# A selective-scan kernel: every fourth product delta\*u\*B by a broadcast load and GpSimd, in place of TensorE and VectorE

## The chip, the cores and the metric

The kernel runs on one core of one Trainium2 chip. The metric is device time in microseconds of one execution of the whole program. Three timed runs of the kernel before gave 1536.02 us as the median (1535.4 to 1540.58).

## The reference: what is computed

For 4096 tokens of width 256, float32 throughout:

```python
xn = layernorm(x)
left, right = split(layernorm(xn)*gamma + beta) @ W_up + b_up        # 128 channels each
u     = silu(causal_conv3(left));  delta = softplus(u @ W_delta + b_delta)
Bm, Cm = u @ W_B, u @ W_C                                             # 64 states each
# for every token t, channel d, state n:
h[d,n] = exp(delta[d]*A[d,n]) * h[d,n] + (delta[d]*u[d]) * Bm[n]      # recurrence over t
y[d]   = sum_n h[d,n] * Cm[n]
s = xn + ((y + u*D) * silu(right)) @ W_down + b_down
g = silu(top-2-of-8 mixture of experts of xn, hidden width 1024)
out = x + s * g
```

The recurrence has 128 x 64 independent sequences over 4096 steps.

## The kernel before, in words

**Pairs and chunks.** The 4096 tokens are cut into 8 chunks of 512 (numbered 0 to 7). Two of the 128 channels times 64 states fill the 128 partitions, so a chunk has 64 pairs of channels, and the main loop runs over 512 pairs `s`. For each pair:

1. ScalarE's queue loads delta of the two channels, each row repeated over 64 partitions, by a broadcast DMA from DRAM (`load_delta`, line 530, three pairs ahead). ScalarE writes exp(delta\*A) to one of two PSUM banks (line 614).
2. TensorE "spreads" delta\*u of the two channels over the partitions: one 128x512 matmul of a 0/1 matrix `pick` with `stack`, which holds delta\*u in two parts (`spread`, line 1117), to one of two PSUM banks `du_bank`. VectorE multiplies that by B (`mult`, line 866), into one of two slots of `b_ring`.
3. VectorE scans: h = a\*h + b along the 512 tokens (`scan`, line 876), into a ring of 8.
4. GpSimd multiplies h by C (`state_by_c`, line 394), into a ring of 8. For 14 pairs of chunk 0 VectorE does it (line 912).
5. TensorE sums over the states, four pairs at a time (`reduce_quad`, line 1052).

**Experts.** The mixture of experts is cut into 39 tiles of 256 rows, 35 of them live with this data. A tile is nine "turns": one that transposes its rows (line 1089) and eight steps. In a step TensorE makes gate and up (line 1105) and three steps later the output product (line 1074, `LAG = 3`); ScalarE makes tanh and a copy (lines 551, 553); VectorE the gated half (line 888); GpSimd the product `hid` (line 409). After each tile ScalarE evicts the sum (line 560) and GpSimd scatters it by two indirect DMAs (line 415). A schedule written out in Python, `BY_PAIR`, gives each pair its turns: 315 live turns over pairs 62 to 483, so three pairs of four have one; from pair 484 on the four dead tiles, up to two turns per pair, with a tiny matmul (line 1041) in place of the products but ScalarE, VectorE and GpSimd working as before.

**The next chunk's inputs** are made meanwhile, at fixed places of a chunk's 64 pairs: convolution at 11 to 13, silu at 16 to 18, softplus and the split of delta\*u at 19 to 29, all mostly on VectorE (lines 709 to 762); at 32 SyncE stores them to DRAM (`store_parts`, five DMAs), at 36 it loads `stack`. The previous chunk's y is gated at pair 5 and projected down at 6 to 10 (lines 895 to 904, 1061).

**Order.** Each engine executes its instructions in the order written. At pair `s` VectorE does mult(s), scan(s-1), then the gated half of pair s-1's turn; TensorE does spread(s+1), a reduction when s%4 is 3, then the turn; GpSimd does state_by_c(s-1), then `hid` of pair s-1's turn and, once per tile, the scatters; ScalarE does load_delta(s+3), exp(s), then its part of the turn. All waits are on semaphores.

Of the kernel before, what the change touches and what calls it, by code (L numbers as in the profile page):

```python
# [6 lines left out]
P = 128  # L7
T, D, E, I, N = 4096, 256, 8, 1024, 64
NT = T // P
CH = 512  # L10
NC = T // CH
TC = CH // P
PAIRS = P // 2
# [66 lines left out]
BY_PAIR = turns_by_pair()  # L80


def state_on_vector(s):

    return s % 4 == 2 and s < 2 * NT - SCATTERS_FIRST
# [19 lines left out]
def mamba_and_experts(nc, x, gam, bet, w_up, b_up, conv_w, conv_b, w_dl, b_dl, w_b2, w_c2, a_log,  # L105
                      dvec, w_dn, b_dn, gate, w_all, c_ident, c_upper, c_pick, c_win, c_first,
                      c_start, c_token, out):
    with ExitStack() as ctx:
# [3 lines left out]
        def sem(name):  # L112
            return ctx.enter_context(nc.semaphore(name))

        x_sorted = nc.dram_tensor("x_sorted", [TILES * SLOT, ROW], F32).ap()
        results = nc.dram_tensor("results", [2 * T + PADS * P, D], F32).ap()
        delta_d = nc.dram_tensor("delta_d", [P, T], F32).ap()
        parts_d = nc.dram_tensor("parts_d", [2, P, T], F32).ap()
        tails_d = nc.dram_tensor("tails_d", [P, 2, T], F32).ap()

# [62 lines left out]
        def stage(name):  # L183

            return spare[:, dict(cv=0, dlt=0, thl=1, ud=1, thr=2, sr=2, u=3, hi=3, ex=4, ln=5, lo=5, wm=6, du=6)[name], :]

        def of_chunk(rep, c, at):

            return rep[:, :, :].rearrange("p c t -> p (c t)")[:, c * (CH + 2) + at:c * (CH + 2) + at + CH]

        def cols(c):

            return slice(c * CH, (c + 1) * CH)
# [32 lines left out]
        s_dp, s_bc, s_bcev, s_sp, s_dlt = (sem(k) for k in ("s_dp", "s_bc", "s_bcev", "s_sp", "s_dlt"))  # L226
        s_partd = sem("s_partd")
        s_stack = [sem("s_stack0"), sem("s_stack1")]
        s_dl = [sem(f"s_dl{i}") for i in range(D_RING)]
        s_tails, s_sel, s_exp, s_bm, s_scan = (sem(k) for k in ("s_tails", "s_sel", "s_exp", "s_bm", "s_scan"))  # L230
        s_carry, s_hc, s_hcv, s_red, s_gt2, s_gated = (sem(k) for k in ("s_carry", "s_hc", "s_hcv", "s_red", "s_gt2", "s_gated"))
# [10 lines left out]

        CONSTS = 19
        KD = 7
        STORES = 16 * 5

        def ge(eng, s, n):

            if n > 0:
                eng.wait_ge(s, n)  # L250
# [5 lines left out]
        def _(sp):  # L256
# [22 lines left out]
            def store_parts(c):  # L279

                sp.wait_ge(s_dlt, (c + 1) * KD)
                sp.dma_start(delta_d[:, cols(c)], stage("dlt")).then_inc(s_partd, 16)
                for n, name in enumerate(("hi", "lo")):
                    sp.dma_start(parts_d[n, :, cols(c)], stage(name)).then_inc(s_partd, 16)
                sp.dma_start(tails_d[:, 0, cols(c)], stage("sr")).then_inc(s_partd, 16)
                sp.dma_start(tails_d[:, 1, cols(c)], stage("ud")).then_inc(s_partd, 16)

            def load_stack(c):

                sp.wait_ge(s_partd, STORES * (c + 1))  # L290
                ge(sp, s_sel, PAIRS * (c - 1))
                for n in range(2):
                    sp.dma_start(stack[64 * n:64 * n + 64, c % 2, :, :].bitcast(F32),
                                 parts_d[n, :, cols(c)].rearrange("(j c) t -> c j t", c=64)).then_inc(s_stack[c % 2], 16)
# [17 lines left out]
            for s in range(PAIR_COUNT):  # L312
                c, at = s // PAIRS, s % PAIRS
                if at == TAILS_AT:
                    sp.wait_ge(s_lr, NC)
                    ge(sp, s_dn, 2 * c)
                    sp.dma_start(tails[:, :, :], tails_d[:, :, cols(c)]).then_inc(s_tails, 16)
                for name, cc, r in work_at(s):
                    if name == "store":
                        store_parts(cc)  # L320
                    elif name == "stack":
                        load_stack(cc)
                if s == MOE_FIRST - 8:
                    sp.wait_ge(s_ytr, NC)
                    sp.wait_ge(s_table, 1)
                    load_weights(0)
                for turn, i, k in BY_PAIR[s]:
                    if turn == "step" and k == 0 and i:
                        load_weights(i)
                if s == (NC - 1) * PAIRS + 12:  # L330
                    sp.wait_ge(s_bm, (NC - 1) * PAIRS)
                    sp.wait_ge(s_hc, states((NC - 1) * PAIRS - 1, False))
                    sp.wait_ge(s_partd, STORES * NC)
                    for c in range(NC):
                        sp.dma_start(x_again[c], x[0, cols(c), :].rearrange("(n p) c -> p n c", p=P)).then_inc(s_again, 16)
# [29 lines left out]
        def _(pool):  # L365
# [21 lines left out]
            def state_by_c(s):  # L387

                c = s // PAIRS
                if s % PAIRS == 0:  # L390
# [3 lines left out]
                pool.tensor_tensor(p_ring[:, s % P_RING, :], h_ring[:, s % H_RING, :], of_chunk(c_rep, c, 2),  # L394
                                   ALU.mult).then_inc(s_hc, 1)

            def bias_rows(c):

                pool.wait_ge(s_scat, 16 * 2 * NT)
                rows = xn[:, c * TC:(c + 1) * TC, 0:D]  # L400
                pool.tensor_tensor(rows, rows, bdn[:, :].unsqueeze(1).broadcast_to([P, TC, D]), ALU.add).then_inc(s_bias, 1)
# [26 lines left out]
            for s in range(PAIR_COUNT):  # L428
                if s:
                    if not state_on_vector(s - 1):  # L430
                        state_by_c(s - 1)
                    after_turns(BY_PAIR[s - 1])
                if s + SCATTERS_FIRST < 2 * NT:
                    scatter_x(s + SCATTERS_FIRST)
                if s % PAIRS == BIAS_AT:
                    bias_rows(s // PAIRS)
            state_by_c(PAIR_COUNT - 1)
# [11 lines left out]
        def _(act):  # L449
# [83 lines left out]
            def load_rows(i):  # L533
# [3 lines left out]
                act.dma_start(xg[:, :, :], x_sorted[rows, 0:D].rearrange("(s p) c -> p s c", p=P)).then_inc(s_xg, 16)  # L537
                act.dma_start(goal[:, i, :, :], x_sorted[rows, D:ROW].rearrange("(s p) c -> p s c", p=P)).then_inc(s_xg, 16)

            def evict_rows(i):  # L540

                act.wait_ge(s_tr, i + 1)
                act.activation(xgT[:, i % 2, :, :].rearrange("p h t -> p (h t)"), bank_of(("rows", i, 0))[:, :], ACT.Copy
                               ).then_inc(s_xgT, 1)
# [64 lines left out]
            for s in range(PAIR_COUNT):  # L609
                if s + D_RING - 1 < PAIR_COUNT:  # L610
                    load_delta(s + D_RING - 1)
                act.wait_ge(s_dl[s % D_RING], 16 * (s // D_RING + 1))
                ge(act, s_scan, s - 1)
                act.activation(a_bank[s % 2][:, :], dl_ring[:, s % D_RING, :], ACT.Exp,  # L614
                               scale=a_neg[:, s % PAIRS:s % PAIRS + 1]).then_inc(s_exp, 1)
                if s % 2 == 0 and s <= 2 * (NC - 2):
                    evict_halves(s // 2 + 1)
                if s % 2 == 1 and s <= 2 * (NC - 2) - 1:
                    evict_columns(s // 2 + 2)
                for name, c, r in work_at(s):  # L620
                    if name == "tanh":
                        tanhs(c)
                    elif name == "log":
                        softplus(c, 1 + r)
                if s % 4 == 1 and s >= 5:
                    save_carry((s - 5) // 4)
                if s == MOE_FIRST - 2:
                    act.wait_ge(s_scat, 16 * 2 * NT)
                    load_rows(0)
                turns(BY_PAIR[s])  # L630
# [12 lines left out]
        def _(v):  # L643
# [215 lines left out]
            def mult(s):  # L859

                c = s // PAIRS
                if s % PAIRS == 0:
                    v.wait_ge(s_bcev, 2 * c + 1)
                v.wait_ge(s_sel, s + 1)
                ge(v, s_scan, s - B_RING + 1)
                v.tensor_tensor(b_ring[:, s % B_RING, :], du_bank[s % 2][:, :], b_rep[:, cols(c)], ALU.mult).then_inc(s_bm, 1)  # L866

            def scan(s):

                q = s % PAIRS  # L870
                v.wait_ge(s_exp, s + 1)
                v.wait_ge(s_bm, s + 1)
                ge(v, s_hc, states(s - H_RING, False))
                ge(v, s_hcv, states(s - H_RING, True))
                ge(v, s_carry, (s - H_RING) // 4 + 1)
                v.tensor_tensor_scan(out=h_ring[:, s % H_RING, :], data0=a_bank[s % 2][:, :],  # L876
                                     data1=b_ring[:, s % B_RING, :], initial=carry[:, q:q + 1],
                                     op0=ALU.mult, op1=ALU.add).then_inc(s_scan, 1)

            def gates(here):  # L880
# [32 lines left out]
                                ).then_inc(s_hcv, 1)  # L913

            for s in range(PAIR_COUNT):
                mult(s)
                if s > 1 and state_on_vector(s - 2):
                    state_by_c(s - 2)
                if s:
# [39 lines left out]
        def _(pe):  # L959
# [151 lines left out]
            def spread(s):  # L1111

                c, g, i16 = s // PAIRS, s % 4, (s % PAIRS) // 4
                if s % PAIRS == 0:
                    pe.wait_ge(s_stack[c % 2], 32 * (c // 2 + 1))
                ge(pe, s_bm, s - 1)
                pe.matmul(du_bank[s % 2][:, :], pick[:, QUADS * (g % 2) + i16, :], stack[:, c % 2, g // 2, :],  # L1117
                          start=True, stop=True).then_inc(s_sel, 1)

            def bank_free(n):  # L1120
# [31 lines left out]

            spread(0)
            for s in range(PAIR_COUNT):
                if s + 1 < PAIR_COUNT:
                    spread(s + 1)
                if s % 2 == 0 and s <= 2 * (NC - 2):
                    left_right(s // 2 + 1)
# [49 lines left out]
```

## Time and profile before

| | |
|---|---|
| median of three timed runs | 1536.02 us |
| the profiled execution's own time | 1538.84 us |
| span of its trace | 1537.0 us |
| TensorE busy (matmuls) | 1252.3 us, 81% |
| VectorE busy | 1284.9 us, 84% |
| GpSimd busy | 1024.5 us, 67% |
| ScalarE busy | 721.0 us, 47% |
| mean share of the 16 DMA engines, data moved | 241.04 MB, 157 GB/s |
| mean granted TensorE clock | 0.887 |

The scan of the first pair starts at 102.8 us, that of pair 64 at 273.7, that of pair 484 at 1390.3 and that of the last one at 1461.0; before lie the normalisations and the routing, behind it a tail of output work. In the views PE is TensorE, PEld its weight loads, DVE VectorE, ACT ScalarE, POOL GpSimd, SP SyncE; "q" behind an engine is a DMA issued from its queue. A bracket at the end of a timeline row is the engine's idle time before the row, and what ended it. An engine's busy time is of its instructions from start to end; neighbours overlap by some tens of nanoseconds, so the pace of an engine is read from start to start.

### The profile page before, as it was taken

The page shows a single profiled execution, that of the slowest core. Times are in us where ns is not written, and L with a number is a line of the kernel's source. Part 1 is how long each engine was busy: PE and PEld are TensorE (multiplying, and loading weights), DVE is VectorE, ACT ScalarE, POOL GpSimd, SP SyncE. Part 2 cuts the span into 40 slices and gives each one's busy share as a digit, 9 for nine tenths or more (in the row PEclk, how much of TensorE's full clock was granted, in tenths as well). Part 3 has the DMA queues.
Part 4 walks back from the last instruction along what each step waited for, and adds up shares of the span by engine and source line. Part 5 has one row for each costly group of instructions (what it writes and reads, how often), then busy time and mean ns, then how long its engine had stood idle before and what let it go on. Part 6 is the DMA issues. An engine that isn't in the chain of part 4 may idle for free. (4 is left out here: it accounts for less than half of the span.)

```text
span 1537.0 us, 21330 instructions
## 1 busy us (share of the span) xinstructions
PE 1252.3 (81%) x5608; PEld 883.0 (57%) x5608; DVE 1284.9 (84%) x1709; ACT 721.0 (47%) x1557; POOL 1024.5 (67%) x976
## 2 busy tenths in 40 slices
PE   5747655888988999899999999889988999897820
PEld 5613111666665677667666676656766777675510
DVE  6545999889888988899888988899888988888838
ACT  1444533454444555454545545454545455455611
POOL 0233788667776677767776667767775777688852
PEclk7569655899999999999999999999999999997555
DMA  9843697445473457436444744636644574744336
GB/s 241 163 124 89 167 284 199 118 124 151 128 212 113 126 142 212 131 106 211 153 133 142 212 129 126 203 97 171 183 137 115 147 227 121 222 143 120 111 120 218
DMA packets 155842, 241.04 MB, mean 157 GB/s; under 512 B 26624, under 2 KB 68224, under 8 KB 155712
## 3 DMA queue, kind: packets, MB, share of 16 engines
q10 hardware_dynamic: 94944, 144.56, 34.3%
q1 hardware_dynamic: 53952, 76.31, 16.4%
q0 software_dynamic: 6816, 18.69, 3.2%
q8 instruction: 51, 0.84, 0.2%
q14 instruction: 79, 0.65, 0.1%
HBM read 195.84 MB, written 43.66 MB: 156 GB/s over the span
## 5 line engine op out<-in xcount | busy, mean ns | idle before, releaser
L394 POOL TENSOR_TENSOR arena<-arena,c_rep 128x512 f32<-128x512 f32 x498 | 593.5, 1196 | 331.3 <-DVE arena L876 316.1
L876 DVE TENSOR_TENSOR_SCAN arena<-bank,carry,arena 128x512 f32<-128x512 f32 x512 | 651.9, 1273 | 28.6 <-ACT bank L614 28.5
L1105 PE MATMUL bank<-xgT,wring 128*128 128x256 f32 x2240 | 533.3, 381 | 8.0 <-DVE xn L904 5.4
L1105 PEld LDWEIGHTS bank<-xgT,wring 128*128 128x128 f32 x2240 | 425.4, 191 | 74.2 <-DVE xn L904 5.8
L614 ACT ACTIVATE bank<-arena,a_neg 128x512 f32<-128x512 f32 x512 | 354.9, 693 | 181.9 <-DVE arena L876 93.6
L866 DVE TENSOR_TENSOR arena<-bank,b_rep 128x512 f32<-128x512 f32 x512 | 350.6, 685 | 48.3 <-PE bank L1117 31.6
L1117 PE MATMUL bank<-stack,pick 128*128 128x512 f32 x512 | 288.1, 581 | 84.6 <-DVE arena L866 64.8
L1074 PE MATMUL bank<-wring,hid 128*128 128x256 f32 x1120 | 300.5, 391 | 43.2 <-ACT o_sb L560 43.2
L551 ACT ACTIVATE th<-bank 128x256 f32<-128x256 f32 x312 | 119.6, 383 | 460.5 <-PE bank L1105 394.0
L1074 PEld LDWEIGHTS bank<-wring,hid 128*128 128x128 f32 x1120 | 206.2, 191 | 145.8 <-issue 105.8
L409 POOL TENSOR_TENSOR hid<-gt,ue 128x256 f32<-128x256 f32 x312 | 249.4, 800 | 32.7 <-DVE gt L888 30.6
L888 DVE SCALAR_TENSOR_TENSOR gt<-th,bank 128x256 f32<-128x256 f32 x312 | 126.9, 407 | 119.8 <-ACT th L551 89.9
L1117 PEld LDWEIGHTS bank<-stack,pick 128*128 128x128 f32 x512 | 105.1, 206 | 168.6 <-DVE arena L866 126.1
L1052 PE MATMUL bank<-arena,win 128*32 128x512 f32 x1024 | 156.3, 686 | 1.9 <-POOL arena L394 1.9
L553 ACT ACTIVATE ue<-bank 128x256 f32<-128x256 f32 x312 | 117.8, 378 | 2.9 <-POOL hid L409 2.9
L415 POOL DMA_INDIRECT results<-o_sb,goal x78 | 77.9, 999 | 26.0 <-issue 16.4
L384 POOL DMA_INDIRECT x_sorted<-xn,route x64 | 65.0, 1015 | 38.7 <-DVE xn L839 25.5
L1041 PEld LDWEIGHTS bank<-ident 128*128 128x128 f32 x136 | 32.5, 309 | 33.9 <-issue 32.4
L1052 PEld LDWEIGHTS bank<-arena,win 128*32 128x32 f32 x1024 | 21.2, 114 | 45.1 <-issue 33.0
L1041 PE MATMUL bank<-ident 128*128 128x2 f32 x136 | 31.1, 330 | 18.3 <-POOL hid L409 14.8
L370 POOL TENSOR_SCALAR pick<-hid,mask 128x2048 fp32r<-128x2048 f32 x2 | 10.9, 5454 | 45.2 <-DVE mask L692 45.2
L1061 PE MATMUL bank<-wdn,tails 128*128 128x256 f32 x64 | 20.3, 448 | 23.6 <-DVE tails L897 12.6
(147 smaller groups left out, 726.9 us busy)
## 6 DMA issues: line engine op xcount, KB each, us to landing
arena<-delta_d ACTq DMA_DIRECT2D x512, 256.0 KB, 3.8
wring<-in_w_all SPq DMA_DIRECT2D x64, 384.0 KB, 4.8
x_sorted<-arena SPq DMA_DIRECT2D x2, 5031.0 KB, 37.5
xg<-x_sorted ACTq DMA_DIRECT2D x39, 256.0 KB
arena<-results SPq DMA_DIRECT2D x16, 512.0 KB, 6.9
xn<-in_x SPq DMA_DIRECT2D x4, 1024.0 KB, 9.5
parts_d<-spare SPq DMA_DIRECT2D x16, 256.0 KB
tails_d<-spare SPq DMA_DIRECT2D x16, 256.0 KB
```

Source lines behind the costliest of these rows:

```text
L394: pool.tensor_tensor(p_ring[:, s % P_RING, :], h_ring[:, s % H_RING, :], of_chunk(c_rep, c, 2), ALU.mult).then_inc(s_hc, 1)
L409: pool.tensor_tensor(hid[:, k % 4, :], gt[:, k % 2, :], ue[:, k % 2, :], ALU.mult).then_inc(s_hid, 1)
L551: act.activation(th[:, :], bank[:, 0:SLOT], ACT.Tanh, scale=0.5).then_inc(s_th, 1)
L553: act.activation(ue[:, k % 2, :], bank[:, SLOT:2 * SLOT], ACT.Copy).then_inc(s_ue, 1)
L614: act.activation(a_bank[s % 2][:, :], dl_ring[:, s % D_RING, :], ACT.Exp, scale=a_neg[:, s % PAIRS:s % PAIRS + 1]).then_inc(s_exp, 1)
L866: v.tensor_tensor(b_ring[:, s % B_RING, :], du_bank[s % 2][:, :], b_rep[:, cols(c)], ALU.mult).then_inc(s_bm, 1)
L876: v.tensor_tensor_scan(out=h_ring[:, s % H_RING, :], data0=a_bank[s % 2][:, :], data1=b_ring[:, s % B_RING, :], initial=carry[:, q:q + 1], ...
L888: v.scalar_tensor_tensor(out=gt[:, k % 2, :], in0=th[:, :], scalar=1.0, in1=bank_of((turn, i, kk))[:, 0:SLOT], op0=ALU.add, op1=ALU.mult). ...
L1052: ins = pe.matmul(y_bank[32 * g:32 * g + 32, :], win[:, 30 - 2 * i:62 - 2 * i], p_ring[:, (4 * q + g) % P_RING, :], start=(i == 0), stop=( ...
L1074: ins = pe.matmul(o_bank[:, s * D:(s + 1) * D], hid[:, k % 4, s * P:(s + 1) * P], wring[:, r, 4 * P:WROW], start=(r == 0 and s == 0), stop ...
L1105: ins = pe.matmul(bank[:, m * SLOT:(m + 1) * SLOT], wring[:, kk, (2 * m + h) * P:(2 * m + h + 1) * P], xgT[:, i % 2, h, :], start=(h == 0) ...
L1117: pe.matmul(du_bank[s % 2][:, :], pick[:, QUADS * (g % 2) + i16, :], stack[:, c % 2, g // 2, :], start=True, stop=True).then_inc(s_sel, 1)
```

## The change

For pairs with s%4 == 3 from chunk 1 on (112 of the 512 pairs):

- no `spread` on TensorE and no `mult` on VectorE;
- ScalarE's queue loads delta\*u of the two channels, broadcast over 64 partitions each, from a new DRAM tensor `du_d` into one of two free 2 KB slots of the arena, five pairs ahead and ahead of exp(s) (`load_du`);
- GpSimd multiplies the slot by B in place (`product_by_b`), two pairs ahead, behind the turn's `hid` and scatters;
- the scan of such a pair waits for GpSimd and reads that slot.

The other 400 pairs keep their course, with ring slots and banks counted over themselves. `store_parts` has a sixth DMA of 256 KB (chunk 0 too).

```diff
+def on_pool(s):
+    return s >= PAIRS and s % 4 == 3
+POOL_PAIRS = [s for s in range(PAIR_COUNT) if on_pool(s)]
+TENSOR_PAIRS = [s for s in range(PAIR_COUNT) if not on_pool(s)]
+ORDER = {s: n for group in (POOL_PAIRS, TENSOR_PAIRS) for n, s in enumerate(group)}
...
+        def product_with_b(s):
+            return ring[:, 22 + ORDER[s] % 2, :] if on_pool(s) else b_ring[:, ORDER[s] % B_RING, :]
...
-        STORES = 16 * 5
+        STORES = 16 * 6
...
+                sp.dma_start(du_d[:, cols(c)], stage("du")).then_inc(s_partd, 16)
...
+            def product_by_b(s):
+                n, c = ORDER[s], s // PAIRS
+                pool.wait_ge(s_bcev, 2 * c + 1)
+                pool.wait_ge(s_du[n % 2], 16 * (n // 2 + 1))
+                pool.tensor_tensor(product_with_b(s), product_with_b(s), b_rep[:, cols(c)], ALU.mult).then_inc(s_bp, 1)
...
                 if s + SCATTERS_FIRST < 2 * NT:
                     scatter_x(s + SCATTERS_FIRST)
+                if s + 2 < PAIR_COUNT and on_pool(s + 2):
+                    product_by_b(s + 2)
...
+            def load_du(s):
+                n, c, ch = ORDER[s], s // PAIRS, 32 * (s % 4) + 2 * ((s % PAIRS) // 4)
+                act.wait_ge(s_partd, STORES * (c + 1))
+                if n > 1:
+                    act.wait_ge(s_scan, POOL_PAIRS[n - 2] + 1)
+                act.dma_start(product_with_b(s), du_d[ch:ch + 2, cols(c)].unsqueeze(0).broadcast_to([N, 2, CH])
+                              ).then_inc(s_du[n % 2], 16)
...
                 if s + D_RING - 1 < PAIR_COUNT:
                     load_delta(s + D_RING - 1)
+                if s + 5 < PAIR_COUNT and on_pool(s + 5):
+                    load_du(s + 5)
...
-                v.wait_ge(s_sel, s + 1)
-                ge(v, s_scan, s - B_RING + 1)
-                v.tensor_tensor(b_ring[:, s % B_RING, :], du_bank[s % 2][:, :], b_rep[:, cols(c)], ALU.mult).then_inc(s_bm, 1)
+                n = ORDER[s]
+                v.wait_ge(s_sel, n + 1)
+                if n >= B_RING:
+                    v.wait_ge(s_scan, TENSOR_PAIRS[n - B_RING] + 1)
+                v.tensor_tensor(product_with_b(s), du_bank[n % 2][:, :], b_rep[:, cols(c)], ALU.mult).then_inc(s_bm, 1)
...
-                v.wait_ge(s_bm, s + 1)
+                v.wait_ge(s_bp if on_pool(s) else s_bm, ORDER[s] + 1)
...
-                                     data1=b_ring[:, s % B_RING, :], initial=carry[:, q:q + 1],
+                                     data1=product_with_b(s), initial=carry[:, q:q + 1],
...
-                mult(s)
+                if not on_pool(s):
+                    mult(s)
...
-                if s + 1 < PAIR_COUNT:
+                if s + 1 < PAIR_COUNT and not on_pool(s + 1):
                     spread(s + 1)
```

## Rows read from the trace of the kernel before

**Rows 1.** The page's costliest groups; busy us, mean ns | idle before, releaser.

```profile
L394 POOL TENSOR_TENSOR arena<-arena,c_rep 128x512 f32<-128x512 f32 x498 | 593.5, 1196 | 331.3 <-DVE arena L876 316.1
L866 DVE TENSOR_TENSOR arena<-bank,b_rep 128x512 f32<-128x512 f32 x512 | 350.6, 685 | 48.3 <-PE bank L1117 31.6
L1117 PE MATMUL bank<-stack,pick 128*128 128x512 f32 x512 | 288.1, 581 | 84.6 <-DVE arena L866 64.8
```

**Rows 2.** Windows: stretch, length, busy PE, PEld, DVE, ACT, POOL, PEclk, DMA, GB/s.

```profile
708.90:747.20 38.30, 36.30 (x180) 27.68 (x181) 33.23 (x43) 20.05 (x47) 30.47 (x30) 1.00 0.79 259
784.90:829.70 44.80, 40.22 (x196) 30.48 (x194) 38.88 (x52) 20.73 (x47) 30.54 (x32) 1.00 0.36 107
829.70:875.60 45.90, 40.89 (x187) 28.25 (x187) 43.63 (x53) 26.17 (x55) 30.44 (x30) 1.00 0.72 205
875.60:913.30 37.70, 36.36 (x177) 27.22 (x176) 33.26 (x45) 19.23 (x44) 27.62 (x30) 1.00 0.57 162
1390.30:1462.00 71.70, 55.90 (x224) 37.70 (x222) 60.17 (x86) 43.70 (x108) 61.68 (x64) 0.57 0.38 115
```

**Rows 3.** Timeline of TensorE's matmuls in a plain stretch; start us, us, engine, line.

```profile
787.94 0.58 PE L1117 MATMUL bank<-stack,pick 128*128 128x512 f32 x1
788.36 1.03 PE L1074 MATMUL bank<-wring,hid 128*128 128x256 f32 x4
789.22 1.89 PE L1105 MATMUL bank<-xgT,wring 128*128 128x256 f32 x8
790.76 0.58 PE L1117 MATMUL bank<-stack,pick 128*128 128x512 f32 x1
```

**Rows 4.** Timeline of TensorE's weight loads in the same stretch.

```profile
787.91 0.19 PEld L1117 LDWEIGHTS bank<-stack,pick 128*128 128x128 f32 x1
788.13 0.85 PEld L1074 LDWEIGHTS bank<-wring,hid 128*128 128x128 f32 x4
789.00 1.70 PEld L1105 LDWEIGHTS bank<-xgT,wring 128*128 128x128 f32 x8
```

**Rows 5.** Timeline of VectorE where it runs without a gap.

```profile
826.43 0.42 DVE L888 SCALAR_TENSOR_TENSOR gt<-th,bank 128x256 f32<-128x256 f32 x1
826.77 0.68 DVE L866 TENSOR_TENSOR arena<-bank,b_rep 128x512 f32<-128x512 f32 x1
827.37 1.27 DVE L876 TENSOR_TENSOR_SCAN arena<-bank,carry,arena 128x512 f32<-128x512 f32 x1
828.56 0.67 DVE L719 SCALAR_TENSOR_TENSOR spare<-spare 128x512 f32<-128x512 f32 x1
```

**Rows 6.** Waits of the whole program: us in total, times, longest us.

```profile
DVE gt L888 <- ACT th L551: 89.9, 97, 1.8
PE bank L1117 <- DVE arena L866: 64.8, 61, 2.5
DVE gt L888 <- ACT ue L553: 27.6, 19, 2.4
PE bank L1041 <- POOL hid L409: 14.8, 8, 3.5
```

**Rows 7.** Lines 394 and 712 alone: duration ns min/median/max, first and last start us.

```profile
L394 POOL TENSOR_TENSOR arena<-arena,c_rep x498: 1080/1263/1637, 104.2 to 1466.1; 128x512 f32<-128x512 f32 x166
L712 DVE SCALAR_TENSOR_TENSOR spare<-c_rep,half,spare x16: 725/746/2572, 70.1 to 1162.7; 128x512 f32<-128x512 f32 x16
```

**Rows 8.** Timeline of GpSimd after a tile's scatters.

```profile
714.56 1.01 POOL L415 DMA_INDIRECT results<-o_sb,goal  x1 [0.16 <-issue]
715.88 0.96 POOL L415 DMA_INDIRECT results<-o_sb,goal  x1 [0.30 <-issue]
716.86 3.85 POOL L394 TENSOR_TENSOR arena<-arena,c_rep 128x512 f32<-128x512 f32 x3
720.67 0.72 POOL L409 TENSOR_TENSOR hid<-gt,ue 128x256 f32<-128x256 f32 x1
```

**Rows 9.** DMA issues: KB each, median us to landing; and the queue of ScalarE.

```profile
arena<-delta_d ACTq DMA_DIRECT2D x512, 256.0 KB, 3.8
q10 hardware_dynamic: 94944, 144.56, 34.3%
```

**Rows 10.** Timeline of ScalarE and its DMA issues in a plain stretch.

```profile
730.08 0.39 ACT L551 ACTIVATE th<-bank 128x256 f32<-128x256 f32 x1 [1.36 <-PE bank L1105]
730.08 0.52 ACTq L530 DMA_DIRECT2D arena<-delta_d  x1
730.71 0.69 ACT L614 ACTIVATE bank<-arena,a_neg 128x512 f32<-128x512 f32 x1
```

**Rows 11.** Waits: TensorE's start of the first pair.

```profile
PE bank L1117 <- DMA stack<-parts_d: 19.6, 1, 19.6
```

More of the change, by code:

```diff
@@ L80, with spreads_until @@
 BY_PAIR = turns_by_pair()
+def on_pool(s):
[3 more added lines that the diff above has]
+ORDER = {s: n for group in (POOL_PAIRS, TENSOR_PAIRS) for n, s in enumerate(group)}
+def spreads_until(s):
+    return sum(p < s for p in TENSOR_PAIRS)
 def state_on_vector(s):
@@ L117, in mamba_and_experts @@
         delta_d = nc.dram_tensor("delta_d", [P, T], F32).ap()
+        du_d = nc.dram_tensor("du_d", [P, T], F32).ap()
         parts_d = nc.dram_tensor("parts_d", [2, P, T], F32).ap()
@@ L228, in mamba_and_experts @@
         s_stack = [sem("s_stack0"), sem("s_stack1")]
+        s_du = [sem("s_du0"), sem("s_du1")]
+        s_bp = sem("s_bp")
         s_dl = [sem(f"s_dl{i}") for i in range(D_RING)]
@@ L290, in load_stack @@
                 sp.wait_ge(s_partd, STORES * (c + 1))
-                ge(sp, s_sel, PAIRS * (c - 1))
+                ge(sp, s_sel, spreads_until(PAIRS * (c - 1)))
                 for n in range(2):
@@ L330, in _ @@
                 if s == (NC - 1) * PAIRS + 12:
-                    sp.wait_ge(s_bm, (NC - 1) * PAIRS)
+                    sp.wait_ge(s_bm, spreads_until((NC - 1) * PAIRS))
+                    sp.wait_ge(s_bp, (NC - 1) * PAIRS - spreads_until((NC - 1) * PAIRS))
                     sp.wait_ge(s_hc, states((NC - 1) * PAIRS - 1, False))
@@ L1115, in spread @@
                     pe.wait_ge(s_stack[c % 2], 32 * (c // 2 + 1))
-                ge(pe, s_bm, s - 1)
-                pe.matmul(du_bank[s % 2][:, :], pick[:, QUADS * (g % 2) + i16, :], stack[:, c % 2, g // 2, :],
+                ge(pe, s_bm, ORDER[s] - 1)
+                pe.matmul(du_bank[ORDER[s] % 2][:, :], pick[:, QUADS * (g % 2) + i16, :], stack[:, c % 2, g // 2, :],
                           start=True, stop=True).then_inc(s_sel, 1)
```

## The prediction

> **What bounds the kernel now.** I read the costliest groups first. Per pair VectorE has a scan and a mult and GpSimd one product; for the same 128x512 product GpSimd takes 1196 ns where VectorE's mult takes 685 [rows 1]. The whole-program shares (VectorE 84%, TensorE 81%, GpSimd 67%) don't say who sets the pace, so I read the windows next. I cut a chunk into four quarters of 16 pairs, by the scans' starts. The rows show chunk 4's first three quarters, chunk 3's third, and the last 28 pairs [rows 2]. Three kinds of stretch come out.
>
> - *Plain quarters* (pairs 32 to 63 of a chunk; 38 us): TensorE busy 36.4 of 37.7 us, VectorE 33.3. TensorE sets the pace.
> - *Second quarters* (pairs 16 to 31, with silu and split; 45.9 us): VectorE busy 43.6, TensorE 40.9. VectorE sets the pace.
> - *First quarters* (44.8 us): TensorE 40.2, VectorE 38.9. They take turns.
> - *The end* (pairs 484 to 511, 71.7 us): GpSimd 61.7, VectorE 60.2, TensorE 55.9. No engine is full, but GpSimd is the fullest.
>
> The waits agree: VectorE waited 89.9 us for the tanh behind TensorE's gate product, TensorE 64.8 us for mults, and TensorE 14.8 us for `hid` of GpSimd [rows 6].
>
> **What is removed.** *112 mults.* The busy row says 685 ns, but where VectorE runs without a gap a mult starts at 826.77 and its scan at 827.37: it holds the engine 0.60 us [rows 5]. That is 4 x 0.60 = 2.4 us in a quarter. Ceiling over all: 112 x 0.60 = 67 us.
> *112 spreads.* Busy 581 ns each [rows 1], but matmuls overlap. From spread to spread it is 790.76 - 787.94 = 2.82 us for a spread and twelve other weights [rows 3]; those twelve take 0.85 + 1.70 = 2.55 us of weight loads [rows 4]. So a spread costs 0.27 us of pace (bounds 0.19, its weight load, and 0.58, its busy time). 4 x 0.27 = 1.1 us in a quarter.
>
> **What is added.** *112 products on GpSimd.* In place in the arena times B is not in the trace. The nearest is line 394, the same shape: 1080 to 1637 ns, median 1263 [rows 7]. I take 1.27, so 5.1 us in a quarter. Room for it: a plain quarter of an odd chunk has GpSimd busy 30.5 of 38.3 us and would have 35.5; of an even chunk 27.6 of 37.7, then 32.7; a second quarter 30.4 of 45.9, then 35.5; the end 61.7 of 71.7, then 61.7 + 7 x 1.27 = 70.6 [rows 2]. (Line 394 is slower in odd chunks, whose C slice starts elsewhere; I don't know which the product resembles, so I take the slow one.)
> *The new wait*, scan(s+2) on the product. The product is issued behind state_by_c(s-1), `hid` and, once a tile, two scatters. After scan(s-1) ends GpSimd needs 1.27 + 0.73 + 1.27 = 3.3 us; VectorE reaches scan(s+2) some three paces less one scan later, 3 x 2.4 - 1.3 = 5.9 us. Slack is 2.6 us. A tile's scatters take 716.86 - 714.56 = 2.3 us and leave three states in a row behind them [rows 8], which uses that slack up, once in twelve pairs. Queued behind a waiting scan are VectorE's gated half and the next mult, and through them TensorE. I charge 3 us for all these in 37 tiles; bounds 0 (the product never falls behind the scatters) and 37 x 1.27 = 47 us.
> *Shared access.* VectorE's line 712 takes 725 ns at best and up to 2572 [rows 7]; in the second quarter some ten such operations with two SBUF inputs run beside GpSimd, and GpSimd's share grows by 5.1/45.9 = 11%. Ten operations prolonged by about half a microsecond in 11% of cases: 0.6 us per second quarter. The mult that goes reads PSUM and one SBUF tile and kept to 685 ns on the mean beside a busy GpSimd [rows 1]. Bounds 0 and 2 us a quarter.
> The Trainium skill, GPSIMD Engine Reference, section Specifications, says that GpSimd shares its SBUF interface with VectorE and that they contend where a VectorE instruction has two SBUF inputs; by that the mults never suffered, the stage work does, and the trace agrees (725 ns against 2572).
> *112 loads* of 256 KB. The 512 like them are most of a queue at 34.3% of the DMA engines [rows 9], so these add at most 112/512 x 34.3 = 7.5 points to a share that stood at 0.36 to 0.79 [rows 2]. They are issued five pairs, some 12 us, ahead and land in 3.8 [rows 9]: hidden. If a load were late, the product would be, as above. Issue takes 0.52 us of ScalarE's queue ahead of exp [rows 10]: where tanh sets ScalarE's pace, exp begins 0.63 us after tanh now, and with two issues about 1.05 after. There VectorE has no mult between the gated half and scan(s) (pair s+1 is GpSimd's), so scan(s) waits for exp: VectorE's saving is lost in exactly the places where TensorE sets the pace anyway. In second quarters VectorE is the late one, and exp is ready. Price taken 0 beyond this; bounds 0 and 112 x 0.45 = 50 us, the upper if exp were always last.
> *A sixth store* per chunk: at chunk 0 TensorE waits for the stores and the stack, 19.6 us [rows 11]; five become six, I take +0.9 us (bounds 0 and 3.8, one landing [rows 9]). In later chunks four pairs lie between store and load: nothing.
>
> **The sum.**
> - Second quarters of chunks 1 to 6: 6 x (2.4 - 0.6) = -10.8.
> - First quarters of chunks 1 to 7: between 1.1 (TensorE) and 2.4 (VectorE); I take 1.2 since TensorE is the fuller: 7 x 1.2 = -8.4.
> - Plain quarters of chunks 2, 4, 6: 6 x 1.1 = -6.6.
> - Plain quarters of chunks 1, 3, 5 and the second of 7: GpSimd would stand at 35.5 of some 37 us, so I take only 0.3 each: 7 x 0.3 = -2.1.
> - The end: 7 x 1.27 = 8.9 us come upon an engine with 10.0 us of gaps, which are waits inside a loop with VectorE and ScalarE; half is taken to show: +4.2.
> - Scatters +3, start +0.9.
>
> In all -19.8. Of the profiled execution's 1538.84 us that leaves 1519.0; that execution stands 2.8 us above the median, so 1536.02 - 19.8 = 1516 us is the forecast.
>
> **Rivals.** *B, VectorE everywhere:* its 97 waits for tanh would shrink with it, since both engines only wait for each other; then up to 112 x 0.60 = 67 us go, 1469. Against it: in plain quarters TensorE has 1.3 us of gaps in 37.7. Chance 0.08.
> *C, nothing measurable* (within 0.5% = 7.7 us, about what a measurement of this kernel tells from no change): only the second quarters gain, and end, scatters and odd chunks give it back: -10.8 + 4.2 + 3 + 0.9 = -2.7, 1533. Chance 0.18.
> *D, slower: GpSimd's queue becomes the bound.* Place: the ops behind a tile's scatters, and the end. GpSimd is already late there: VectorE's 19 waits for `ue`, 27.6 us [rows 6], are ScalarE waiting for `hid`. If each tile's backlog now grows by a product, 37 x 1.27 = 47 us come against the 28 of gains: +19 and 4 at the end, about 1560. It decides once GpSimd's busy share in plain quarters passes about 95%; the odd ones would be at 35.5/37. Chance 0.16.
> The Trainium skill, GPSIMD Engine Reference, section Engine selection, advises VectorE for elementwise products because GpSimd is about twice as slow with two inputs. Here the trace has 1196 against 685 ns; the rule would make D the forecast if GpSimd had no idle time, and rows 2 show 7 to 15 us of it a quarter.
> *The forecast*, A: 0.58.
>
> **Range and chances.** A's own range is 1500 to 1530: the first and plain quarters at VectorE's 2.4 give 12 us more, the scatters' and the end's costs 12 less. For 8 in 10 the range goes to 1496 below, and to 1543 above, which takes in C and D's near half. Faster by over 0.5%: 0.55 of A and B's 0.08, 0.63; the same: the rest of A and most of C, 0.20; slower: D and a little, 0.17.
>
> **What the changed profile would show.** VectorE's busy time lower by about 112 x 0.685 = 77 us, GpSimd's higher by about 142. Second quarters about 44 us in place of 45.9, plain even ones about 36.6, plain odd ones still near 38, the end near 76. GpSimd's share in odd plain quarters above 90%. Waits of the scan on GpSimd's product: few, near scatters. Waits of the scan on exp grow in plain quarters. I am wrong if scans wait for products throughout (D), if plain quarters shrink by over 2 us (B), or if the product takes 1.1 us or 1.6 in place of 1.27.

## The result, and the profile after

The changed kernel took 1527.56 us at the median of five runs (1518.2 to 1529.25), beside 1540.58 us (1535.4 to 1541.87) for the kernel before on the same chip: ratio 0.9907, 95% interval 0.9882 to 0.9932. It is faster by 0.9%, 13 us between the medians and 14 by the ratio; 19.8 us were forecast. The spans of the two profiled executions are 1537.0 and 1524.3 us, 12.7 us apart, and this difference can be followed stretch by stretch.

The page after, the costliest groups that answer to [rows 1], and the new one (line 420 is the old 394, 914 the old 866, 1166 the old 1117; line 428 is the new product):

```profile
L420 POOL TENSOR_TENSOR arena<-arena,c_rep 128x512 f32<-128x512 f32 x498 | 595.5, 1202 | 183.9 <-DVE arena L924 177.8
L914 DVE TENSOR_TENSOR arena<-bank,b_rep 128x512 f32<-128x512 f32 x400 | 272.3, 681 | 40.4 <-PE bank L1166 32.4
L1166 PE MATMUL bank<-stack,pick 128*128 128x512 f32 x400 | 234.7, 598 | 73.3 <-DVE arena L914 51.9
L428 POOL TENSOR_TENSOR arena<-arena,b_rep 128x512 f32<-128x512 f32 x112 | 142.6, 1273 | 0.1
```

The product takes 1273 ns, as assumed, and GpSimd stood idle before all 112 of them for 0.1 us together: their loads were never late. VectorE lost 350.6 - 272.3 = 78.3 us of mults, but its busy time as a whole fell by only 62.6 us (1284.9 to 1222.3): other operations of it took longer. GpSimd's rose by 129.8 us (1024.5 to 1154.3).

Windows of the changed kernel; the first four are the stretches of [rows 2] (pairs 224 to 239, 256 to 271, 272 to 287, 288 to 303), the last is the end, up to the start of the last scan (in [rows 2] it runs 1.0 us further):

```profile
704.60:742.20 37.60, 35.78 (x178) 27.23 (x179) 30.08 (x40) 19.52 (x45) 35.49 (x35) 1.00 0.92 293
778.30:824.60 46.30, 41.36 (x193) 30.97 (x191) 38.33 (x48) 20.75 (x47) 36.46 (x37) 0.96 0.43 127
824.60:868.50 43.90, 40.47 (x190) 28.71 (x190) 39.61 (x49) 25.61 (x54) 35.71 (x34) 1.00 0.77 235
868.50:903.90 35.40, 33.86 (x168) 25.47 (x167) 30.54 (x40) 19.61 (x45) 31.70 (x34) 1.00 0.73 214
1374.90:1447.70 72.80, 52.14 (x217) 34.97 (x215) 55.14 (x79) 44.12 (x108) 68.38 (x72) 0.60 0.43 134
```

Plain quarters and the second one are shorter, the first is longer (46.30 for 44.80 us), and GpSimd is now busy 35.49 of 37.60 us in a plain odd quarter. The first three columns are summed over chunks 1 to 6, from the scans' starts in each trace; the end runs from the start of scan 484 to that of the last (us):

| kernel | first quarters | second | plain | end |
|---|---|---|---|---|
| before | 275.1 | 283.4 | 464.6 | 70.7 |
| changed | 292.1 | 267.7 | 450.2 | 72.8 |
| changed, once more | 289.9 | 270.0 | 450.9 | 72.8 |
| changed, gating in PSUM | 277.5 | 267.4 | 452.4 | 72.8 |

Each line of the table is one execution. First quarters scatter by some us from trace to trace without the change too: four variants of the kernel before, described below, have 274.2 to 279.1.

So second and plain quarters gave 30.1 us and first quarters took 17.0 back. Of these, 15.0 lie in pairs 4 to 8 of a chunk, where the previous chunk's y is gated (in us; "wait" is TensorE's for the second operation of the gating, ahead of the down projection):

| chunk | that operation: before, changed | wait: before, changed | pairs 4 to 8: before, changed, gating in PSUM |
|---|---|---|---|
| 1 | 0.94, 1.36 | 2.6, 3.2 | 13.0, 13.4, 11.9 |
| 2 | 1.10, 2.55 | 1.6, 4.1 | 12.6, 16.7, 13.7 |
| 3 | 1.28, 3.49 | 1.8, 4.1 | 12.7, 17.9, 12.2 |
| 4 | 0.69, 2.50 | 0.0, 0.1 | 13.0, 14.0, 13.3 |
| 5 | 0.95, 0.95 | 1.0, 1.5 | 12.7, 12.7, 12.5 |
| 6 | 0.73, 2.40 | 2.3, 4.2 | 13.2, 17.6, 14.8 |

The loss is large in chunks 2, 3 and 6, where the operation is prolonged and TensorE waits over 4 us for it; small in chunk 4, where the operation takes 2.50 us but TensorE is late itself; none in chunk 5, where no product stands in that row. Chunk 3's five pairs, the kernel before, the changed one, and within the latter a stretch of 5 us:

```profile
626.00:638.80 12.80, 9.43 (x46) 6.65 (x45) 12.39 (x17) 4.98 (x11) 7.44 (x8) 1.00 0.39 120
```

```profile
616.50:634.40 17.90, 12.21 (x44) 7.90 (x43) 13.86 (x16) 5.01 (x11) 10.67 (x11) 0.81 0.34 103
623.00:628.00 5.00, 5.00 (x16) 2.33 (x15) 3.93 (x5) 0.69 (x1) 4.18 (x4) 0.50 0.03 10
```

The timeline of the changed kernel there, VectorE, GpSimd and TensorE one after another:

```profile
617.67 0.66 DVE L943 TENSOR_TENSOR tails<-bank,tails 128x512 f32<-128x512 f32 x1
618.37 3.49 DVE L945 TENSOR_TENSOR tails<-tails 128x512 f32<-128x512 f32 x1
621.78 0.68 DVE L914 TENSOR_TENSOR arena<-bank,b_rep 128x512 f32<-128x512 f32 x1
...
618.15 0.72 POOL L442 TENSOR_TENSOR hid<-gt,ue 128x256 f32<-128x256 f32 x1
618.83 1.25 POOL L420 TENSOR_TENSOR arena<-arena,c_rep 128x512 f32<-128x512 f32 x1
620.05 1.25 POOL L428 TENSOR_TENSOR arena<-arena,b_rep 128x512 f32<-128x512 f32 x1
...
622.00 2.05 PE L1110 MATMUL bank<-wdn,tails 128*128 128x256 f32 x4 [4.06 <-DVE tails L945]
624.41 1.94 PE L1101 MATMUL bank<-arena,win 128*32 128x512 f32 x8
626.27 2.04 PE L1123 MATMUL bank<-wring,hid 128*128 128x256 f32 x4
628.14 1.90 PE L1154 MATMUL bank<-xgT,wring 128*128 128x256 f32 x8
```

Read from above. Line 945 is the second operation of the gating (y times silu, then plus u\*D), with both inputs in SBUF. It begins under a `hid`, and behind that GpSimd runs state and product without a pause, until 621.30; line 945 ends at 621.86. TensorE waits for it 4.06 us ahead of the down projection. From 621.4 us, still within that wait, until 628.1 us the granted clock is 0.50, which is 1.2 GHz of 2.4, and four output matmuls take 2.04 us where such four took 1.03 [rows 3]. Then VectorE waits for the tanh behind them (3.9 us). In the kernel before GpSimd has one operation there, and TensorE waits 1.75 us:

```profile
627.90 1.28 DVE L897 TENSOR_TENSOR tails<-tails 128x512 f32<-128x512 f32 x1
...
627.36 1.27 POOL L394 TENSOR_TENSOR arena<-arena,c_rep 128x512 f32<-128x512 f32 x1 [1.06 <-DVE arena L876]
...
629.32 1.10 PE L1061 MATMUL bank<-wdn,tails 128*128 128x256 f32 x4 [1.75 <-DVE tails L897]
```

The same line over both traces:

```profile
L897 DVE TENSOR_TENSOR tails<-tails x8: 691/948/1276, 284.3 to 1470.1; 128x512 f32<-128x512 f32 x8
```

```profile
L945 DVE TENSOR_TENSOR tails<-tails x8: 691/1881/3493, 282.6 to 1457.5; 128x512 f32<-128x512 f32 x8
```

The waits of the changed kernel that answer to [rows 6], and those for exp (28.5 us in 43 times before):

```profile
DVE gt L936 <- ACT th L595: 65.9, 57, 4.0
PE bank L1166 <- DVE arena L914: 51.9, 44, 2.6
DVE gt L936 <- ACT ue L597: 63.7, 44, 3.1
PE bank L1090 <- POOL hid L442: 13.8, 8, 5.0
DVE arena L924 <- ACT bank L660: 69.9, 94, 2.9
```

### The profile page after: what moved, and what is told of

Its sections match the earlier page's. It is cut to its first block and busy times, and to the rows that moved or that the text cites. A ratio compares the mean times of both kernels' runs of the same rounds, so it can differ in the third digit from the quotient of the medians.

```text
span 1524.3 us, 21337 instructions
## 1 busy us (share of the span) xinstructions
PE 1222.2 (80%) x5496; PEld 860.7 (56%) x5496; DVE 1222.3 (80%) x1597; ACT 721.6 (47%) x1557; POOL 1154.3 (76%) x1088
## 3 DMA queue, kind: packets, MB, share of 16 engines
q1 hardware_dynamic: 55104, 78.41, 16.7%
## 5 line engine op out<-in xcount | busy, mean ns | idle before, releaser
L924 DVE TENSOR_TENSOR_SCAN arena<-bank,carry,arena 128x512 f32<-128x512 f32 x512 | 651.9, 1274 | 75.2 <-ACT bank L660 69.9
L914 DVE TENSOR_TENSOR arena<-bank,b_rep 128x512 f32<-128x512 f32 x400 | 272.3, 681 | 40.4 <-PE bank L1166 32.4
L1166 PE MATMUL bank<-stack,pick 128*128 128x512 f32 x400 | 234.7, 598 | 73.3 <-DVE arena L914 51.9
L442 POOL TENSOR_TENSOR hid<-gt,ue 128x256 f32<-128x256 f32 x312 | 244.9, 786 | 38.3 <-DVE gt L936 34.9
L936 DVE SCALAR_TENSOR_TENSOR gt<-th,bank 128x256 f32<-128x256 f32 x312 | 126.3, 405 | 132.1 <-ACT th L595 65.9
L1166 PEld LDWEIGHTS bank<-stack,pick 128*128 128x128 f32 x400 | 83.3, 209 | 141.6 <-DVE arena L914 96.3
L428 POOL TENSOR_TENSOR arena<-arena,b_rep 128x512 f32<-128x512 f32 x112 | 142.6, 1273 | 0.1
L1110 PE MATMUL bank<-wdn,tails 128*128 128x256 f32 x64 | 24.2, 519 | 31.3 <-DVE tails L945 20.6
L1101 PEld LDWEIGHTS bank<-arena,win 128*32 128x32 f32 x1024 | 21.2, 114 | 49.2 <-issue 36.2
```

The costliest lines, as they stand in the source:

```text
L428: pool.tensor_tensor(product_with_b(s), product_with_b(s), b_rep[:, cols(c)], ALU.mult).then_inc(s_bp, 1)
L442: pool.tensor_tensor(hid[:, k % 4, :], gt[:, k % 2, :], ue[:, k % 2, :], ALU.mult).then_inc(s_hid, 1)
L914: v.tensor_tensor(product_with_b(s), du_bank[n % 2][:, :], b_rep[:, cols(c)], ALU.mult).then_inc(s_bm, 1)
L936: v.scalar_tensor_tensor(out=gt[:, k % 2, :], in0=th[:, :], scalar=1.0, in1=bank_of((turn, i, kk))[:, 0:SLOT], op0=ALU.add, op1=ALU.mult). ...
L1101: ins = pe.matmul(y_bank[32 * g:32 * g + 32, :], win[:, 30 - 2 * i:62 - 2 * i], p_ring[:, (4 * q + g) % P_RING, :], start=(i == 0), stop=( ...
L1166: pe.matmul(du_bank[ORDER[s] % 2][:, :], pick[:, QUADS * (g % 2) + i16, :], stack[:, c % 2, g // 2, :], start=True, stop=True).then_inc(s_ ...
```

## The experiments

Twelve runs, each timed beside the kernel before. A count of us for a kind of quarter is of chunks 1 to 6 in one profiled execution, so it is less sure than a ratio. Theory: the new product prolongs one operation of the gating, TensorE stands still and its clock falls. Rivals: GpSimd is late in general; the added load delays exp.

**Gating through PSUM.** VectorE's product goes back to PSUM, so that neither operation has two SBUF inputs.

```diff
-                v.tensor_tensor(gated, y_bank[:, :], tails[:, 0, :], ALU.mult).then_inc(s_gt2, 1)
+                v.tensor_tensor(y_bank[:, :], y_bank[:, :], tails[:, 0, :], ALU.mult).then_inc(s_gt2, 1)
-                v.tensor_tensor(gated, gated, tails[:, 1, :], ALU.add).then_inc(s_gated, 1)
+                v.tensor_tensor(gated, y_bank[:, :], tails[:, 1, :], ALU.add).then_inc(s_gated, 1)
-                    ge(pe, s_gt2, q // QUADS)
+                    ge(pe, s_gated, q // QUADS)
```

> The changed kernel, with the gating of a chunk done through PSUM (y_bank = y_bank * silu in place, then gated = y_bank + u*D part), so that no VectorE operation of it has two SBUF inputs. Theory 1 (the new GpSimd product stands back to back with state_by_c while VectorE's second gating operation wants the shared access; it took 3.49 us, TensorE idled 4.1 us and its granted clock fell to 0.50): the second gating operation takes 0.68 us in all chunks, first quarters of chunks 1 to 6 fall from 292 us to about 270, the whole to 18 to 25 us less than the changed kernel, ratio to the kernel before about 0.978. Rival 1 (GpSimd's queue is late in general, hid behind the product): the gating becomes short but first quarters stay above 285 us, ratio 0.989. Rival 2 (the load's issue delays exp): no change, 0.9907.

1511.21 us, ratio 0.9812 (0.9797 to 0.9827). First quarters fell to 277.5 us, within 2.4 of the kernel before. About 270 us and a ratio of 0.978 were expected, so the direction is theory 1's and the size falls short; rival 1 had them above 285 us. The same line, and the same five pairs of chunk 3, in this trace:

```profile
L945 DVE TENSOR_TENSOR tails<-bank,tails x8: 690/691/692, 283.7 to 1445.2; 128x512 f32<-128x512 f32 x8
```

```profile
614.40:626.60 12.20, 9.30 (x44) 6.57 (x43) 11.08 (x16) 5.01 (x11) 10.58 (x11) 1.00 0.51 151
```

In all eight chunks the operation takes 0.69 us, in seven of them beside a busy GpSimd, and in chunk 3 the clock stays at 1.00 after a wait of 1.27 us. In chunks 2 and 6 TensorE still waits 2.3 and 2.5 us, and a stretch of 3.4 us at 0.50 follows; there the pairs kept 1.2 and 1.6 us of their loss. The Trainium skill, GPSIMD Engine Reference, section Specifications, names exactly this condition, a VectorE instruction with two SBUF inputs; the traces agree (3493 ns at most with two, 692 with one). This alone is 0.95% of the time. VectorE's waits for exp were 70.1 us, as in the changed kernel (69.9): they stay and the time goes, which rival 2 had excluded. The second operation's own time, in chunks 1 to 6 together, went from 13.3 to 4.1 us. That is 9 of the 14.6 us by which first quarters fell; the other 5 or so are left for what followed it, TensorE's standstill and its clock, and no run takes these two apart.

**No product beside the gating.** `on_pool` leaves out pair 7 of each chunk (`s % PAIRS != 7`), so 105 products.

> The changed kernel, but pair 7 of every chunk stays on TensorE and VectorE (105 products instead of 112), so no product is issued at pair 5, beside the gating. Theory 1: gating's second operation back to 1.28 us at most, first quarters about 275 us, ratio about 0.981. Rival 1: 7 of 112 products fewer changes nothing visible, ratio 0.990. Rival 2: 0.990.

1520.96 us, ratio 0.9869 (0.9852 to 0.9886); first quarters 284.9 us, the operation up to 2273 ns. Half of the way: right in its direction, short in its size. The rest of GpSimd's row, whose phase shifted, still meets the gating.

**Products of two columns.**

```diff
-                pool.tensor_tensor(product_with_b(s), product_with_b(s), b_rep[:, cols(c)], ALU.mult).then_inc(s_bp, 1)
+                pool.tensor_tensor(product_with_b(s)[:, 0:2], product_with_b(s)[:, 0:2], b_rep[:, c * CH:c * CH + 2], ALU.mult).then_inc(s_bp, 1)
```

> The changed kernel with GpSimd's product cut to 2 of 512 columns (B is left out of the rest of those pairs' input): waits, loads and order as they are, GpSimd's 142 us of work gone. Theory 1: as with the gating through PSUM in first quarters, plus what the products cost elsewhere (longer stage operations, the end, waits of ue for hid): ratio about 0.972. Rival 1: all losses go, 0.970, and first quarters fall only here. Rival 2: waits of the scan for exp (69.9 us) stay and with them the time, 0.985 or more.

1510.0 us, ratio 0.9809 (0.9788 to 0.983): no better than the gating in PSUM with the full products. I expected 0.972. The gating's second operation is back at its length of before (at most 1.27 us), and first quarters at 274.8 us; the end is 70.1 us in place of 72.8. With the gating still in SBUF here, worth some 3 us by the kernel before with it in PSUM (below), the 142 us of products cost about 4 us besides the gating (an estimate: 1511.2 - 1510.0 + 3).

**The load behind exp.** `load_du` moved below the activation of exp.

> The changed kernel with the load of delta*u issued behind exp(s) instead of ahead of it. Theory 1: VectorE's waits for exp fall from 69.9 us towards 30, but they lie mostly where TensorE sets the pace; ratio 0.987 to 0.991. Rival 2: the waits for exp are what ate the gain: ratio about 0.975.

1525.28 us, ratio 0.9901 (0.9886 to 0.9917): not told apart from the change itself. The waits for exp went from 69.9 to 58.1 us, not towards 30 as expected, and those for tanh from 65.9 to 82.3. The edit moved too little of the waits to test rival 2 by itself; what speaks against it is the gating through PSUM, which left them whole.

**Gating through PSUM in the kernel before.**

> The kernel before, with the gating through PSUM alone. Theory (the gating's price of access is the change's own, GpSimd's product being the second operation in the row): here the second gating operation takes 0.94 to 1.28 us in five of eight chunks and would take 0.69: 2 to 4 us at most, ratio 0.997 to 1.000. Rival (the gating through PSUM is worth as much without the change): ratio 0.988.

1536.36 us, ratio 0.9978 (0.9967 to 0.9989): as expected, 3 us. Of the 15 us between the change with and without it (0.9907 and 0.9812), 3 were there before, and about 11 are the change's own price.

**One side of the removal at a time.** In the kernel before, for pairs 67, 71, ...:

```diff
-                v.tensor_tensor(b_ring[:, s % B_RING, :], du_bank[s % 2][:, :], b_rep[:, cols(c)], ALU.mult).then_inc(s_bm, 1)
+                w = 2 if s >= PAIRS and s % 4 == 3 else CH
+                v.tensor_tensor(b_ring[:, s % B_RING, 0:w], du_bank[s % 2][:, 0:w], b_rep[:, c * CH:c * CH + w], ALU.mult).then_inc(s_bm, 1)
```

> The kernel before, with the mult of pairs 67, 71, ... cut to 2 of 512 columns (those pairs' input is left out), all else as it was. Theory (VectorE sets the pace in second quarters, TensorE in plain ones): second quarters of chunks 1 to 6 fall from 283 to about 268 us, first and plain ones by little, ratio 0.986 to 0.990. Rival (VectorE's time counts everywhere): all quarters fall, ratio 0.981 as with the whole change and the gating mended.

1534.94 us, ratio 0.997 (0.9956 to 0.9984). Second quarters of chunks 1 to 6 fell from 283.4 to 272.4 us, plain ones stayed (464.1). The places are as expected, the size is not: 268 us and a ratio of 0.986 to 0.990 were expected. The profiled execution (1530.38 us) is also 4.6 us below the median of its kind, so the 11.0 us may be too many. First quarters went up by 1.9.

> The kernel before, with the spread of the same pairs cut to 2 of 512 columns (its weight load stays), all else as it was. Theory (TensorE sets the pace in plain quarters): plain quarters of chunks 1 to 6 fall from 465 us by 4 to 10, second quarters stay at 283, ratio 0.993 to 0.997. Rival (VectorE's time counts everywhere): nothing, 1.000.

(The same cut of the spread's columns.) 1535.12 us, ratio 0.9974 (0.9961 to 0.9986). Plain quarters 460.5 us, second ones 282.7: TensorE's work counts in plain quarters, VectorE's in second ones. The ratio lies just short of the expected range, and first quarters went up by 4.0 us (279.1).

> The kernel before with both the mult and the spread of pairs 67, 71, ... cut to 2 columns, weight loads and hand-offs kept. Theory (two works with places of their own: VectorE's in second quarters, TensorE's in plain ones, where the weight load of 0.19 us is most of a spread's price and stays): the sum of the two single ones, about -9 us, ratio 0.994. Rival (both engines wait for each other, and only taking work from both at once frees them): much more than the sum, ratio 0.982 or less.

1529.39 us, ratio 0.9945 (0.9924 to 0.9965): the sum of the two (0.3% and 0.26%), so the rival falls. Plain quarters 459.7 us. Second ones are at 277.1, a gain of only 6.3 us where the mults alone had shown 11.0: so far do single executions differ.

**The new side left out**, gating in PSUM kept: no loads, products or waits for them.

> The changed kernel with the gating through PSUM, and the new side left out: no load of delta*u, no product, no wait for it (the scans of those pairs read zeros). No spread, weight load or mult either for those pairs. Theory: GpSimd's products and the loads cost 3 to 10 us (waits for hid and exp, longer stage operations, the end), so ratio 0.974 to 0.979 against 0.981 with them. Rival (what is left is TensorE's and VectorE's own): 0.981, the new side costs nothing once the gating is mended. If weight loads are what a spread costs, plain quarters of chunks 1 to 6 stay near 451 us.

1499.18 us, ratio 0.9748 (0.9729 to 0.9768). Against 0.9812 the whole new side costs 0.64%, 10 us (the two ratios are of different sets of runs; the changed kernel gave 0.9907 and 0.9919 in two such sets); 3.4 of them lie at the end (69.4 for 72.8), 8.5 in first quarters (269.0 for 277.5). Plain quarters are 450.5 us with or without products. Between 459.7 (both cut to two columns) and 450.5 lie 9.2 us for 48 spreads, 0.19 each: as much as a spread's weight load [rows 4]. The hand-offs, and the two-column mults, went in the same step and weren't separated from it. Products of two columns had kept the loads, their issue and the scans' waits, and took 1510.0 us; with the gating's 3 us taken off, some 6 or 7 us lie in those (an estimate). No run leaves out the loads alone, so which of them it is stays open.

**Products made twice.**

```diff
+                pool.tensor_tensor(dump[:, :], product_with_b(s), b_rep[:, cols(c)], ALU.mult)
                 pool.tensor_tensor(product_with_b(s), product_with_b(s), b_rep[:, cols(c)], ALU.mult).then_inc(s_bp, 1)
```

> The changed kernel with the gating through PSUM, and every product on GpSimd made twice (the first time into a tile that nothing reads): 112 x 1.27 = 142 us more of GpSimd's time. If GpSimd at 94% of a plain quarter was just short of being the bound (rival D of the prediction), plain quarters grow to 39 to 41 us and the whole comes out above the kernel before, ratio 1.00 to 1.03. If GpSimd has slack that its busy share hides, 0.985.

1574.3 us, ratio 1.0223 (1.0202 to 1.0243). In an odd plain quarter and at the end GpSimd is full:

```profile
755.30:795.50 40.20, 36.40 (x176) 26.77 (x174) 30.85 (x40) 20.00 (x45) 39.39 (x37) 1.00 0.49 159
1417.10:1498.30 81.20, 55.06 (x219) 37.43 (x217) 55.33 (x79) 44.62 (x108) 78.53 (x80) 0.56 0.41 121
```

GpSimd is busy 39.39 of 40.20 us there (98%) and VectorE's waits for `ue` are 97.1 us. Scans now wait 42.9 us for products (36 times; 4.6 us in the change). The mechanism of rival D exists, one product per four pairs further on. Against the gating in PSUM with single products, plain quarters grew by 13.0 us (465.4), first ones by 17.1 (294.6), second ones by 21.2 (288.6) and the end by 8.3.

**All mended.** Gating in PSUM, load behind exp, and no GpSimd pairs from 484 on (`PAIRS <= s < MOE_LIVE`).

> The changed kernel with the gating through PSUM, the load of delta*u behind exp(s), and no GpSimd pairs from pair 484 on (105 products). Theory: the gating's 20 us as before, the end back to about 71 us from 73, the loads' place 0 to 3 us: ratio 0.978 to 0.981, 1506 to 1511 us. Rival (the three share one gain, or the spreads given back to TensorE at the end cost as much): no better than the gating alone, 0.981 or more.

1504.15 us, ratio 0.9774 (0.976 to 0.9788): 2.3% below the kernel before. The gain over the gating alone is 0.38%, 6 us; the end accounts for 1.8 (71.0 for 72.8), first quarters for 5.8 (271.7 for 277.5), where the load's place may count once the gating doesn't hide it (waits for exp 55.0 us in place of 70.1). That wasn't tried apart, and 5.8 us is little more than first quarters scatter by.

**The change once more**, timed in the same set as the kernel with both cuts, the one without the new side and the one with double products:

> The changed kernel itself once more, beside the others of this set: ratio 0.9907 as before, within its interval of 0.9882 to 0.9932, if sets can be compared.

1527.74 us, ratio 0.9919 (0.9901 to 0.9937): within the first interval, so sets can be compared to about 0.1%.

## Why the prediction came out as it did

The forecast was 1516 us, 19.8 less; about 14 came (12.7 between the profiles). Of the 11.6 us between 1516 and 1527.56, 4.6 are the kernel before, timed at 1540.58 here and at 1536.02 there. The direction was right and the time lies inside the stated range, but that it came so near is partly luck: first quarters of chunks 1 to 6 missed by 24 us (-7.2 forecast, +17.0 measured), and second and plain ones by 11 the other way (-19.2 and -30.1). By the steps, profile against profile:

- *Mult at 0.60 us of pace, in second quarters*: -10.8 forecast, 267.7 - 283.4 = -15.7 measured (-13.4 in the other run). Cutting the mults alone gave -11.0, mults and spreads together -6.3. The place was right; the size is of the right order, with executions that differ by several us. The 0.6 us taken off each second quarter for shared access did not show: VectorE's stage operations there took 65.7 us in all, 67.8 before.
- *Spread at 0.27 us of pace*: plain quarters gained 14.4 us for 48 spreads, 0.30 each. Right, and met from both ends: 0.10 for the columns (4.9 us for 48, both cut), 0.19 for the weight load and what went with it. Single quarters gained 0.0 to 2.4 us, and three of twelve passed the 2 us that was to speak for rival B; the mean is 1.2.
- *Odd plain quarters limited by GpSimd*, 0.3 us each: wrong. Those of chunks 1, 3 and 5 gained 8.9 us, more than the even ones (5.5). GpSimd at 94% didn't hold anything up; at 98%, with double products, it did. I took "nearly full" for "the bound".
- *First quarters*, -8.4: wrong, and the step that failed. In chunks 1 to 6 they took 17.0 us more. "Shared access" was priced for the second quarters' stage work alone, at 0.6 us each; the first quarters' gating, with two SBUF inputs as well and TensorE waiting right behind it, was left out. In [rows 7] line 712's 2572 ns showed what such an operation can come to, and that was the same thing, beside three GpSimd operations in a row in the trace before:

```profile
650.76 2.57 DVE L712 SCALAR_TENSOR_TENSOR spare<-c_rep,half,spare 128x512 f32<-128x512 f32 x1
...
649.60 2.49 POOL L394 TENSOR_TENSOR arena<-arena,c_rep 128x512 f32<-128x512 f32 x2
652.05 0.72 POOL L409 TENSOR_TENSOR hid<-gt,ue 128x256 f32<-128x256 f32 x1
```

  The price was the operation itself (7.6 us more in chunks 1 to 6 than before) and what followed it: TensorE without work for 4 us, and then at half its clock. The gating is not all: with it in PSUM, first quarters stood at 277.5 us, without the new side at 269.0. The gain that was forecast for them (7.2 us in chunks 1 to 6) is there when nothing is added (6.1 us). Of the 8.5 us between, 6.3 lie outside pairs 4 to 8; which of product, load and hand-off takes them is open.
- *The new wait*, 3 us: scans waited 4.6 us. Four of the six products stand right behind a scatter, as said. The trace names no releaser for these waits, but each of the six ends within 0.1 us of a product's end (the product of 611.86 us ends at 613.11, the scan starts at 613.20), and the trace before has none of the kind. The totals of the scan's waits:

```profile
  ACT bank L660: 69.9, 94
  issue: 4.6, 6
```

  Waits for `ue`, behind which stands `hid`, rose from 27.6 to 63.7 us. About half of the rise isn't the products': with them cut to two columns it is 45.4 us, and 48.5 in the kernel before with nothing but the mults cut.
- *Loads*: never late, as said. The waits for exp grew from 28.5 to 69.9 us, as said. Issuing the load behind exp gained nothing measurable in the change itself; whether the loads are free once the gating is mended stays open.
- *The end* +4.2, measured 72.8 - 70.7 = +2.1, about half; *start* +0.9, measured +0.7 to the first scan (102.8 to 103.5 us).

Rival B fell (a plain quarter gained 1.2 us on the mean, not 2.4). C and D each saw a part: something did give half of the 30.1 us back, but it was the gating first of all and not GpSimd's lack of time. *Signs*: VectorE's busy time fell by 62.6 us, not 77, and GpSimd's rose by 129.8, not 142; the product took 1.27 us, as assumed.

## What to carry to other kernels

When work moves to GpSimd, list VectorE's operations with two SBUF inputs and ask of each who waits for it: here one such operation lasted as long as GpSimd's unbroken row of work beside it, and the engine behind it paid as well. Writing the intermediate back to PSUM took the operation out of the contention at no cost that shows (0.69 us each). An engine's price for an operation is its start-to-start pace: here 0.30 us for a spread whose busy time is 0.58. An engine busy for 94% of a stretch didn't set its pace here; doubling the load showed how far it was from doing so. And when a total comes near the forecast, the terms are still to be compared one by one: here two large errors had opposite signs.

## What the runs showed of the hardware

VectorE's 128x512 addition with two SBUF inputs took 691 ns alone and 3493 ns when it was issued under the first of three GpSimd operations in a row; it ended 0.56 us after the last. It isn't always VectorE that gives way to the whole row: in chunk 7 of the changed kernel the same addition ended 0.55 us after the first of two (1276 ns), and the product behind that took 1717 ns in place of 1273. What decides between the two wasn't found. With one input from PSUM the addition took 690 to 692 ns in all eight cases, in seven of them with GpSimd busy.

TensorE's waits ahead of the down projection, and the clock behind them: after 4.13, 4.06 and 4.16 us (chunks 2, 3 and 6 of the changed kernel) and 2.62 us (chunk 1, before) it was 0.50 for 6.7 us or more, and in chunk 3 of the changed kernel four 256-column matmul records took 2.04 us in place of 1.03. After 2.29 and 2.45 us (chunks 2 and 6, gating in PSUM) it was 0.50 for 3.4 us; after 2.25 us (chunk 6, before) and 1.27 us (chunk 3, gating in PSUM) it stayed at 1.00.
